# Adjacency stage of a graph network: who marks the rows and who scales them

## The reference, cut to what matters

```python
neigh_sum = jax.ops.segment_sum(x[edge_src], edge_dst, num_segments=n)      # layer 0
...
deg = jax.ops.segment_sum(w, dst_f, num_segments=n)                          # layer 1
norm = dinv[src_f] * w * dinv[dst_f]
agg = jax.ops.segment_sum(h[src_f] * norm[:, None], dst_f, num_segments=n) + b_conv
```

## Time and profile before

| | us |
|---|---|
| median of 3 runs (1926.17 to 1927.8) | 1926.62 |
| the profiled execution, its own time | 1927.84 |
| its span, first to last instruction | 1926.0 |
| lies outside the span | 1.8 |

### The profile page before, as it was taken

The page is one execution under the profiler, slowest core; times in us unless marked ns, Lnnn a source line. Parts: engine busy times, 40 slices in busy tenths (PEclk is TensorE's granted clock), DMA queues, the critical chain, the costliest instruction groups (busy, mean ns, idle before and its releaser), DMA issues. The chain is left out here.

```text
span 1926.0 us, 26185 instructions
## 1 busy us (share of the span) xinstructions
PE 1701.5 (88%) x8051; PEld 1108.9 (58%) x8052; DVE 895.7 (47%) x2244; ACT 542.1 (28%) x1504; POOL 751.2 (39%) x866
## 2 busy tenths in 40 slices
PE   5589988987588888898699997799999999999998
PEld 4134434545477777544344455677677677677675
DVE  7932277345699999788566567100000000000002
ACT  0011101122488888401111134121121122122113
POOL 0577777777788888740111100400000000034005
PEclk9999989999799999999799998899999999999999
DMA  8000092000300000202200042756304400520003
GB/s 250 2 2 2 9 361 59 13 23 13 80 1 0 1 0 0 55 1 85 69 1 0 1 175 116 222 196 240 141 22 191 191 22 16 196 70 16 22 16 118
DMA packets 76225, 144.19 MB, mean 75 GB/s; under 512 B 21809, under 2 KB 23425, under 8 KB 71941
## 3 DMA queue, kind: packets, MB, share of 16 engines
q1 hardware_dynamic: 49415, 118.60, 17.4%
q0 software_dynamic: 18976, 10.95, 2.5%
q10 hardware_dynamic: 7776, 13.97, 2.2%
HBM read 107.75 MB, written 35.69 MB: 74 GB/s over the span
## 5 line engine op out<-in xcount | busy, mean ns | idle before, releaser
L338 POOL DMA_INDIRECT sorted_edges<-fa_records,fa_edge_slot x313 | 312.6, 999 | 155.3 <-issue 100.4
L2058 PEld LDWEIGHTS et_ps_h<-ex_turned,arena 128*128 128x128 f32 x3072 | 348.1, 193 | 21.5 <-issue 21.5
L2058 PE MATMUL et_ps_h<-ex_turned,arena 128*128 128x128 f32 x3072 | 348.4, 276 | 10.3 <-issue 10.3
L2068 PE MATMUL et_ps_y<-arena,et_hidden_t 128*128 x768 | 337.5, 592 | 0.0
L1968 DVE TENSOR_SCALAR ex_turned<-et_ps_t,ex_ln_g,ex_ln_b 128x128 f32<-128x128 f32 x96 | 32.8, 404 | 584.1 <-PE et_ps_t L2038 584.1
L2068 PEld LDWEIGHTS et_ps_y<-arena,et_hidden_t 128*128 128x128 f32 x768 | 142.2, 190 | 160.7 <-issue 160.7
L1054 POOL TENSOR_SCALAR ad_row<-iota,ad_edges 128x128 fp32r<-128x128 f32 x295 | 211.3, 728 | 40.3 <-PE ad_ps L1130 30.7
L1107 ACT ACTIVATE ad_row_high<-ad_row,ad_edges 128x128 fp32r<-128x128 f32 x472 | 184.2, 391 | 50.0 <-DVE ad_row L1076 34.7
L1129 PE MATMUL ad_ps<-ad_to,ad_row_high 128*128 128x320 f32 x472 | 153.0, 336 | 51.2 <-ACT ad_row_high L1107 48.2
L1939 POOL DMA_INDIRECT xn_rows<-slot_out,from_slots x10 | 12.2, 1217 | 475.6 <-POOLq L1936 472.8
L1074 DVE TENSOR_SCALAR ad_to<-iota,ad_edges 128x320 fp32r<-128x320 f32 x472 | 169.7, 419 | 9.8 <-DMA ad_edges<-sorted_edges 9.8
(11 more groups left out here) (399 smaller groups left out, 2155.0 us busy)
## 6 DMA issues: line engine op xcount, KB each, us to landing
arena<-L_ffn_W SPq DMA_DIRECT2D x16, 4096.0 KB, 18.4
slot_rows<-fa_zeros SPq DMA_DIRECT2D x1, 7424.0 KB, 28.0
slot_out<-fa_zeros SPq DMA_DIRECT2D x1, 7168.0 KB, 50.0
slot_out<-et_y ACTq DMA_DIRECT2D x24, 256.0 KB, 2.0
et_rows_in<-slot_rows ACTq DMA_DIRECT2D x24, 256.0 KB, 2.7
sorted_edges<-fa_records,fa_edge_slot POOLq DMA_INDIRECT x313
arena<-x SPq DMA_DIRECT2D x1, 2240.0 KB
neighbour<-fa_Wv SPq DMA_DIRECT2D x10, 224.0 KB
```

Source lines behind the costliest of these rows:

```text
L338: nc.gpsimd.indirect_dma_start(g.sorted_edges, bass.IndirectOffsetOnAxis(ap=self.edge_slot[0:rows, e:e + 1], axis=0), self.records[0:rows, ...
L2058: last = pe.matmul(ps_h[:, f % 2, i, :], x.weights[:, at:at + P], turned[:, k, :], start=(k == 0), stop=(k == KD - 1))
L2068: last = pe.matmul(ps_y[:], hidden_t[:, i, :], x.weights[:, bass.ds(buffer * (2 * HALF) + (HALF + i * D), D)], start=(i == 0), stop=(i == ...
```

## The change

In every group GpSimd makes three row marks and nothing else, VectorE makes one row mark, and ScalarE makes all eight scalings. `pool_rows`, the helper `over_columns`, GpSimd's `scale_low`, the semaphore `low_scaled` and TensorE's wait on it are gone. The column marks, products and adds stay as they are.

```diff
-    POOL_LOW = 1
+    POOL_ROWS = 3
...
-        def pool_rows(t):
-            return 3 - t % 2
...
-                for c in range(pool_rows(t)):
+                for c in range(POOL_ROWS):
                     last = nc.gpsimd.tensor_scalar(row[:, u, c, :], g.iota[:, 0:P], field(t, c, 0), None, ALU.is_equal)
                 last.then_inc(rows_made, 1)
 
-            def scale_low(t, u):
-                pool.wait_ge(columns_made, t + 1)
-                nc.gpsimd.tensor_tensor(row_low[:, u, CHUNKS - POOL_LOW:], row[:, u, CHUNKS - POOL_LOW:].bitcast(F32),
-                                        over_columns(t, POOL_LOW, 3), ALU.mult).then_inc(low_scaled, 1)
-
-            in_turn(build_rows, scale_low, NG, BUFS)
+            for t in range(NG):
+                build_rows(t, t % BUFS)
...
-                for c in range(pool_rows(t), CHUNKS):
+                for c in range(POOL_ROWS, CHUNKS):
                     last = v.tensor_scalar(row[:, u, c, :], g.iota[:, 0:P], field(t, c, 0), None, ALU.is_equal)
...
-                    last = nc.scalar.activation(row_high[:, u, c, :], row[:, u, c, :].bitcast(F32), ACT.Copy, scale=field(t, c, 2))
-                    if c < CHUNKS - POOL_LOW:
-                        nc.scalar.activation(row_low[:, u, c, :], row[:, u, c, :].bitcast(F32), ACT.Copy, scale=field(t, c, 3))
+                    nc.scalar.activation(row_high[:, u, c, :], row[:, u, c, :].bitcast(F32), ACT.Copy, scale=field(t, c, 2))
+                    last = nc.scalar.activation(row_low[:, u, c, :], row[:, u, c, :].bitcast(F32), ACT.Copy, scale=field(t, c, 3))
                 last.then_inc(scaled, 1)
...
                 pe.wait_ge(scaled, t + 1)
-                pe.wait_ge(low_scaled, t + 1)
```

More of the change, by code:

```diff
@@ L1011, in adjacency @@
         weights = totals[:, 0]
-        first_loaded, loaded, columns_made, rows_made, scaled, low_scaled, used, added, chain, arrived = (m.sem(n) for n in (
-            "first_loaded", "loaded", "columns_made", "rows_made", "scaled", "low_scaled", "used", "added", "chain", "arrived"))
+        first_loaded, loaded, columns_made, rows_made, scaled, used, added, chain, arrived = (m.sem(n) for n in (
+            "first_loaded", "loaded", "columns_made", "rows_made", "scaled", "used", "added", "chain", "arrived"))
         block = stack.enter_context(nc.Block())
```

## The result

The changed kernel takes 1912.28 us (median of 4 runs, 1908.57 to 1914.37), the kernel before 1926.66 beside it. The ratio is 0.9922, with a 95% interval of 0.9904 to 0.9941. That is 14.4 us less (15.0 by the ratio) where 10.2 were forecast. The direction held, and ScalarE became the bound as forecast, but the size was too small: the range began at 1912, and 1926.62 x 0.9922 is 1911.6.

A forecast was written before the change was run, and what follows sets the result against it. ScalarE was to bound the adjacency stage: 504.83 + 118 groups x 2.37 + 0.8 hole + 2.44 end = 787.7 us against 797.89, 10.2 less, so a median of 1916.4 us; forecast 1912 to 1922.5, range 1912 to 1926.

The forecast's parts named there:

- ScalarE becomes the bound: Adjacency stage: ScalarE's eight scalings take 2.35 us a group, bounds 2.34 and 2.36, over VectorE's 2.25.
- The friction: Adjacency stage: an estimated 0.02 us a group added because three engines don't fit together, making 2.37.
- VectorE at 2.25: VectorE's need a group: the middle of 2.11 (all 0.24 slowing is the scaling's) and 2.40 (all the marks').
- rival 1: GpSimd's third mark slows VectorE as the scaling did: 2.42 to 2.49 us a group, no change, chance 0.14.
- The row mark: VectorE's row marks, 0.20 us each, fall from 1.5 to 1 a group in the mean.
- GpSimd at 2.19: GpSimd's three row marks a group at the mean of 0.729 us take 2.19, less than ScalarE's 2.35.
- The start and the end: Stage start: a hole of 0.8 us replaces one of 3.08; stage end: 2.44 us behind the last scaling.
- Behind the stage: After the stage: nothing takes the gain back; the clock may move it by a microsecond either way.
- Rival 2: GpSimd becomes the bound, its three marks taking 2.65 us a group: 22.9 us later, 1949.5, chance 0.12.
- Rival 3: A port lock makes GpSimd's and VectorE's marks add up: 3.18 us a group, 2012 us, chance 0.01.
- my signs in the profile: Stage: VectorE waits 0.1 us a group before adds, quartets 1.18 to 1.33, GpSimd mark 0.70 to 0.76, last add 788.
- theory C: From the follow-up runs: VectorE loses some 0.10 us each time a GpSimd instruction begins during VectorE's marks.

The follow-up runs named there:

- e4: Changed kernel, but ScalarE leaves out one of its eight scalings (weight matrix not the reference's): 2.292 us a group, ratio 0.9886.
- e2: Kernel before with only the scaling moved to ScalarE, row marks dealt as before: 2.345 us a group, ratio 0.9916.
- e5: e2 with ScalarE leaving out one of its eight scalings (weight matrix not the reference's), on another chip: 2.338 us a group, ratio 0.9952.
- e9: Kernel before with two row marks a group on GpSimd and two on VectorE, GpSimd's two-input scaling kept: 2.405 us a group, ratio 0.9962.
- e10: e9 with GpSimd's scaling made from one tensor input instead of two: 2.402 us a group, ratio 0.9949.
- e1: Changed kernel measured again, nothing edited: 2.344 us a group, ratio 0.9936 to the kernel before.
- e11: Kernel before measured again, nothing edited: 2.439 us a group, ratio 0.998.
- e12: Changed kernel measured a third time, nothing edited: 2.344 us a group, ratio 0.9915 to the kernel before.
- e3: Kernel before with only the row mark moved: three marks a group on GpSimd, which keeps its scaling: 2.408 us a group, ratio 0.9955.
- e7: Changed kernel with all four row marks on GpSimd and none on VectorE, on another chip: 2.610 us a group, ratio 1.0115.
- e13: e4 with GpSimd also waiting for VectorE's marks of the group before: 2.322 us a group, ratio 0.991.
- e14: Changed kernel with one two-input scaling back on GpSimd in every second group, plus the wait of e13: 2.407 us a group, ratio 0.9967.
- e15: e14 without the wait in front of GpSimd's marks: 2.393 us a group, ratio 0.9953.
- e8: Kernel before with GpSimd's scaling made as comparison and product in one operation, on another chip: 2.592 us a group, ratio 1.009.

## Why the prediction was right or wrong

**ScalarE becomes the bound: right.** It is busy without a gap. Its price was 2.35 with bounds 2.34 and 2.36, and it is 2.344.

**The friction: wrong, and this is the term that was mis-sized.** I added 0.02 a group for three engines that hardly fit together and made it 2.37. There was none; 0.026 x 118 = 3.1 us, which is the 2.7 that the stage gained over the forecast (12.9 against 10.2) and a little. What the runs show in its place: with the longest need of the three, ScalarE did not wait once after the start, and a group took its price and no more, 2.344. That held however close the next engine stood: VectorE needs 0.05 less in the changed kernel (2.292, e4) and only 0.007 less in e2 (2.338, e5), and e2 takes 2.345. The even pattern of the changed kernel is not the reason, for e2's alternates; nor does such a pattern need ScalarE as the bound, for e9 and e10 repeat theirs with VectorE busy all the time. What kept ScalarE's work ready is open. The four sets of buffers would do it, but no run changed their number.

**VectorE at 2.25: near, by luck in part.** It needs 2.292 (e4), 0.04 more. I placed 2.25 beside the group that took 2.21 "beside GpSimd's marks alone", and used that group against rival 1. The trace of the kernel before has this line too, between those of the earlier trace rows:

```profile
646.83 0.40 POOL L1059 TENSOR_TENSOR ad_row_low<-ad_row,ad_edges 128x128 fp32r<-128x128 f32 x1
```

So a scaling reached 0.26 us into that group's first column mark, and then GpSimd stood idle until 647.68: the group was no measure of marks alone. My split of the 0.24 into a scaling's and the marks' part asked for the kind of instruction, and e9 and e10, with two kinds, lose the same.

**The row mark: right in its price, wrong in its share.** I counted 0.10 a group for half a mark (1.5 x 0.20 to 0.20) and never asked what the scaling alone would do. It does everything (e2). The prediction had this in it: by the same middle, half of the 0.24 for the scaling, VectorE with 1.5 row marks would need 2.21 + 0.12 = 2.33, already under ScalarE's 2.35.

**GpSimd at 2.19: near.** 2.02 for three marks, with 0.32 of waiting. The marks became faster in the mean (0.729 to 0.691); one of the three lay under the add each time and took 0.60. VectorE's marks did not fill less of the time, as I had reckoned: (2.344 - 0.73)/2.344 is 69%, against 70% before.

**The start and the end: right.** A hole of 0.85 where 0.8 were reckoned, and 2.44 us from the last scaling's end (781.42 + 0.44) to the last add's (784.30), as forecast.

**Behind the stage: a microsecond allowed, too little.** The first measurement had 1.5 us more than the stage explains; the profiles put such differences behind and before the stage, in kernels of either sort (e1, e11, e12). I allowed a microsecond for the clock; the 17 profiles spread over 5. A range should have held that. The stage's 12.9 alone would have made it 1926.6 - 12.9 = 1913.7, inside the range; what took the first measurement to its edge is not the change.

**The rivals.** Rival 1 (GpSimd's marks cost VectorE as much as the scaling) is out by e4. Rival 2 (GpSimd the bound) is what e3 and e7 made of it, at 2.41 and 2.61. Rival 3, the lock, is out: in e7 GpSimd ran without a gap and made four marks in 2.61 us, while VectorE made four column marks and an add in the same time and waited besides. If each excluded the other, the four marks and the column marks would follow one another, 4 x 0.60 + 1.18 = 3.58 at the least. Both are slowed instead, GpSimd by up to 0.48 in a mark, VectorE by some 0.1. The Trainium skill ("SBUF — State Buffer", Who interferes with whom) says that a VectorE operation in a two-port mode and a GpSimd operation share a port pair, and that the second one is fully blocked for the whole instruction. If VectorE's marks run in that mode, which no run here shows by itself, the trace does not agree.

Of my signs in the profile four did not come. VectorE's waits before its adds are not seen as idle time (0.3 us in all); they probably hide behind the last mark, which stands 0.25 before the add instead of 0.20. The quartets of column marks take 1.35, not at most 1.33. GpSimd's mark has a mean of 0.691, under the 0.70 to 0.76. And the last add ends at 784.30, not at 788.

## What to carry to other kernels

Before moving two things at once, price each move alone: here the scaling's move gave all of the gain and the row mark's none, because the next engine stood 0.1 us away. When several engines are within a few per cent of each other, find out what each needs by taking work off the one that sets the pace (e4, e5): a busy share of 229.66 in 230 us did not show that VectorE had 0.05 a group to spare. Add nothing for friction without a row that shows it: here ScalarE's own price was the pace, even with the next one 0.007 us behind. An extra wait to order the engines cost more here than it gave (e13). And test a count over whole groups against the single instructions before building on it: theory C fitted nine profiles by the group and fails by the mark.

## What the runs showed of the hardware

- Row marks on GpSimd and marks on VectorE slow each other without excluding each other: a GpSimd mark of 0.60 takes up to 1.08 (kernel before, e4), and a column mark of 0.295 takes 0.40 in the mean where it lies wholly beside one (the third in the changed kernel, 402 ns over 98 groups).
- VectorE's loss is 0.09 to 0.30 us a group, the same with a GpSimd scaling of one input or two, 0.69 or 0.39 long (e10 and e9). Divided by the GpSimd instructions that begin beside VectorE's marks it is 0.09 to 0.13 in nine of the profiles and 0.14 to 0.15 in e14 and e15; in e3, where GpSimd is full as well, part of it may be waiting. But the beginning is not what costs: marks in whose time a GpSimd instruction begins take 0.296 in e9, e10 and e13, and the loss falls on others. What decides which mark is delayed is open.
- On GpSimd 128 columns cost 0.40 as a product of two tensors (e9), 0.60 as a comparison with a scalar per partition (before), and 0.79 as comparison and product in one operation with two such scalars (e8), each at its shortest or nearly so.
- The kernel before settled at 2.454 in one profile and at 2.439 in another: a stage in which VectorE sets the pace beside GpSimd can have more than one rhythm. It need not: e9 and e10 repeat one group.
